# Routing one tile behind its product, and one weight piece of the second layer split on GpSimd, in a fused two-layer kernel on Trainium2

## What is computed

```
x = x + ffn0(cond0(x, c))        # layer 0
x = x + ffn1(cond1(x, c, side))  # layer 1
cond0: per batch a 64x64 channel mix, a softmax-weighted sum of 8 matrices, plus a bias
ffn0 : y @ W0.T + LoRA of the top 2 of 8 experts. The gate is
       h = relu(layernorm(y @ gw1.T + gb1)); g = h @ gw2.T + gb2; top 2, softmax of the two.
       An expert that more than 1536 of the 4096 rows choose (first, or second) is switched off.
cond1: grouped convolution over positions (9 taps, 4 groups) plus a context bias
ffn1 : y @ W.T + b + 8 low-rank experts weighted by a softmax of q.k
```

## Time and profile before

| what | value |
|---|---|
| median of three runs | 1320.56 us (1319.37 to 1320.86) |
| the profiled execution | 1316.55 us, span 1314.8 us |
| TensorE busy | 1285.5 us, 98% of the span |
| VectorE, ScalarE, GpSimd busy | 737.5, 279.8, 236.4 us |
| mean granted clock of TensorE | 0.992 of 2.4 GHz |
| DMA queue q1 | 142.25 MB, 40.8% of 16 engines' span |

### The profile page before, as it was taken

How to read it: one execution, slowest core, us unless ns; L and a number is a source line. 1 busy time by engine, 2 the same in 40 slices (tenths; PEclk the granted TensorE clock), 3 DMA queues, 4 the chain that set the end, 5 groups by cost and what they waited for, 6 DMA issues and landing times.

```text
span 1314.8 us, 20627 instructions
## 1 busy us (share of the span) xinstructions
PE 1285.5 (98%) x7223; PEld 1195.6 (91%) x7223; DVE 737.5 (56%) x1727; ACT 279.8 (21%) x515; POOL 236.4 (18%) x173
## 2 busy tenths in 40 slices
PE   9699999999999997999999999999999999999999
PEld 9699999999999996898998998898898898898897
DVE  6878777777777775644444444444444444344332
ACT  6233222223222332311111111111111111111110
POOL 2344232223222311110100100110110110110110
PEclk9899999999999998999999999999999999999999
DMA  8245534343344347453343353353343343353310
GB/s 295 68 148 164 125 125 125 120 123 105 111 130 114 101 152 215 137 113 74 86 112 73 86 109 77 86 106 79 86 104 81 86 105 81 86 102 84 87 49 32
DMA packets 109879, 142.75 MB, mean 109 GB/s; under 512 B 6160, under 2 KB 86416, under 8 KB 109840
## 3 DMA queue, kind: packets, MB, share of 16 engines
q1 hardware_dynamic: 109840, 142.25, 40.8%
HBM read 88.72 MB, written 53.50 MB: 108 GB/s over the span
## 4 chain that ended last, share of the span: by engine, by line
PE 92%; DVE 4%; DMA 2%; issue 1%; POOL 1%; ACT 0%; SPq 0%; DVEq 0%; POOLq 0%; ACTq 0%
PE ps L1170 28%; PE ps L1172 27%; PE ps L1171 27%; PE ps L1311 6%; PE ps L1312 2%; DMA staging<-in_w 1%; DMA x_round<-whole 1%; DVE oh_all L927 0%; DMA z<-in_cpack 0%; DMA row<-in_xr 0%; PE ps L1402 0%; DVE part L896 0%; DVE row L904 0%; POOL xo L596 0%; PE ps L1287 0%
## 5 line engine op out<-in xcount | busy, mean ns | idle before, releaser
L1170 PE MATMUL ps<-weights,lhs_h 128*128 128x512 f32 (+2 forms) x1408 | 498.5, 354 | 0.8 <-issue 0.8
L1172 PE MATMUL ps<-weights,lhs_l 128*128 128x512 f32 (+2 forms) x1408 | 490.2, 348 | 0.0
L1171 PE MATMUL ps<-weights,lhs_h 128*128 128x512 f32 (+2 forms) x1408 | 489.1, 347 | 0.0
L1170 PEld LDWEIGHTS ps<-weights,lhs_h 128*128 128x128 f32 x1408 | 264.7, 188 | 24.0 <-issue 1.1
L1172 PEld LDWEIGHTS ps<-weights,lhs_l 128*128 128x128 f32 x1408 | 264.4, 188 | 20.8
L1171 PEld LDWEIGHTS ps<-weights,lhs_h 128*128 128x128 f32 x1408 | 264.8, 188 | 20.0
L643 POOL TENSOR_TENSOR xo<-row,wsum 128x512 f32<-128x512 f32 x60 | 76.9, 1308 | 663.5 <-DMA out_x<-xo 663.5
L1170 PE MATMUL ps<-weights 128*128 128x396 f32 x384 | 133.4, 347 | 0.1
L1171 PE MATMUL ps<-weights 128*128 128x396 f32 x384 | 132.6, 345 | 0.0
L1172 PE MATMUL ps<-weights 128*128 128x396 f32 x384 | 132.5, 345 | 0.0
L1142 DVE TENSOR_TENSOR xo<-ps,xo 128x512 f32<-128x512 f32 x64 | 43.1, 691 | 148.3 <-PE ps L1172 148.3
(11 more groups left out here) (151 smaller groups left out, 1466.8 us busy)
## 6 DMA issues: line engine op xcount, KB each, us to landing
row<-spill SPq DMA_DIRECT2D x30, 576.0 KB, 5.7
z<-x_round SPq DMA_DIRECT2D x32, 516.0 KB, 3.8
xo<-in_xt SPq DMA_DIRECT2D x32, 512.0 KB, 4.0
out_x<-xo SPq DMA_DIRECT2D x31, 512.0 KB, 2.7
x_round<-row SPq DMA_DIRECT2D x60, 256.0 KB, 5.5
row<-in_xr SPq DMA_DIRECT2D x31, 394.0 KB, 3.5
spill<-row SPq DMA_DIRECT2D x31, 394.0 KB, 4.4
staging<-in_w SPq DMA_DIRECT2D x8, 832.0 KB, 6.3
```

What stands on the lines that cost most here:

```text
L1170: pe.matmul(out_ap, lhs[0], rhs[0], start=first, stop=False, skip_group_check=True)
L1171: pe.matmul(out_ap, lhs[0], rhs[1], start=False, stop=False, skip_group_check=True)
L1172: return pe.matmul(out_ap, lhs[1], rhs[0], start=False, stop=last, skip_group_check=True)
```

## The change

1. In the first phase VectorE and ScalarE route tile t+1 in period t instead of tile t+2. Ahead of the first period only tile 0 is routed. Periods 0 and 1 have an order of their own. In period 24 two tiles, 25 and 26, are routed, and from then on again tile t+2 in period t.
2. SP loads the first part of row t+3 in period t (before: of row t+4), once tile t+1 is routed.
3. In the turn piece N1+4 is split low by GpSimd, behind its first additions of the second phase, and no longer by VectorE. ScalarE makes its high part behind `z_high(0)` instead of before `y_high(30,2)`. SP issues x1_store(0) before `y01[1]` and piece N1+4 before x1_store(1).

```diff
+        CATCH_UP = 24
+        def routed_in(t):
+            if isinstance(t, int) and t >= CATCH_UP:
+                return [t + 1, t + 2] if t == CATCH_UP else [t + 2]
+            return [t + 1]
-        by_pool = (N_LB0, N_CONV, N_LB1, N1)
+        by_pool = (N_LB0, N_CONV, N_LB1, N1, N1 + 4)
 # SP, ahead of the first period
             for u in range(2):
                 sp.wait_ge(mix_read[0], u + 1)
                 spill0(u, u)
-                sp.wait_ge(spilled0[u], 16)
-                sp.wait_ge(counted, u + 1)
-                load_xr0(u + 2, u)
+            sp.wait_ge(spilled0[0], 16)
+            sp.wait_ge(counted, 1)
+            load_xr0(2, 0)
 # SP, phase_a
                 spill0(t + 2, u)
-                if before_end(t, 4):
-                    left, = counts((it + 2) * 16)
-                    sp.wait_ge(spilled0[u], left)
-                    sp.wait_ge(counted, ahead)            # ahead = t + 3
-                    load_xr0(t + 4, u)
+                left, = counts((it + u + 1) * 16)
+                sp.wait_ge(spilled0[1 - u], left)
+                sp.wait_ge(counted, routed)               # routed = t + 2
+                load_xr0(t + AHEAD, 1 - u)
 # SP, the turn
             chunk(N1 + 3)
+            x1_store(0, 0)
             sp.wait_ge(row_ready12, TILES)
             sp.dma_start(y01[1], spill[P:2 * P, ER:ROW]).then_inc(row_in[1], 16)
-            x1_store(0, 0)
             z_load(0, 0, 0)
+            chunk(N1 + 4)
             x1_store(1, 1)
-            chunk(N1 + 4)
 # GpSimd, phase_b, behind its two additions
+                if at(t, 0):
+                    split_lo(N1 + 4)
 # ScalarE: root(1) ahead of the first period goes; phase_a
-                if later(t, 1):
+                if later(t, 2):
                     y_high(t + 2, 0)
                 bias12_of(t + 1)
                 if later(t, 1):
                     y_high(t, 1)
-                root(t + 2)
+                    for r in routed_in(t):
+                        root(r)
                 y_high(t, 2)
                 if before_end(t, XB):
                     x_high(t + XB, b, it + 2)
+                if at(t, 0):
+                    y_high(3, 0)
+                    root(1)
 # ScalarE, the turn
             y_high(TILES - 3, 2)
-            split_hi(N1 + 4)
             y_high(TILES - 2, 2)
             z_high(0)
+            split_hi(N1 + 4)
 # VectorE: route(1, 1) ahead of the first period goes; phase_a
+                if at(t, 0):
+                    mix_matrix(3, 3); y_low(0, 2); evict(0, 0, 1); evict(2, 0, 0); x_low(4, 0)
+                    y_low(3, 0); evict(0, 0, 2); route(1, 1)
+                elif at(t, 1):
+                    y_low(1, 1); mix_matrix(4, 0); route(2, 0); y_low(1, 2); evict(1, 1, 1)
+                    evict(3, 1, 0); x_low(5, 1)
+                else:
                     mix_matrix(t + AHEAD, (b + AHEAD) % XB)
                     y_low(t, 1)
                     evict(t + 2, u, 0)
-                    route(t + 2, u)
+                    for r in routed_in(t): route(r, r % 2)    # in the loop: route(t + 1, 1 - u)
                     y_low(t, 2)
                     evict(t, u, 1)
                     if before_end(t, XB): x_low(t + XB, b)
 # VectorE, the turn
             z_low(0)
             evict(T2, 0, 2)
-            split_lo(N1 + 4)
             conv_read_low(0, 0, 0)
```

More of the change, by code:

```diff
@@ L451, in phase_a @@
                 u = b % 2
-                now, ahead, more = counts(t, t + AHEAD, t + 5)
+                now, routed, ahead, more = counts(t, t + 2, t + AHEAD, t + 5)
                 if later(t, 1):
@@ L463, in phase_a @@
                 spill0(t + 2, u)
-                if before_end(t, 4):
-                    left, = counts((it + 2) * 16)
-                    sp.wait_ge(spilled0[u], left)
-                    sp.sem_inc(passed_sp, 1)
-                    sp.wait_ge(counted, ahead)
-                    sp.sem_inc(passed_sp, 1)
-                    load_xr0(t + 4, u)
+                left, = counts((it + u + 1) * 16)
+                sp.wait_ge(spilled0[1 - u], left)
+                sp.sem_inc(passed_sp, 1)
+                sp.wait_ge(counted, routed)
+                sp.sem_inc(passed_sp, 1)
+                load_xr0(t + AHEAD, 1 - u)
                 if before_end(t, 6):
@@ L747, in _ @@
             bias12_of(0)
-            root(1)
             def phase_a(t, b, it):
-                if later(t, 1):
+                if later(t, 2):
                     y_high(t + 2, 0)
@@ L977, in _, with links_before @@
             route(0, 0)
-            route(1, 1)
-            A_BASE = 2 + AHEAD * MIX_LINKS + (AHEAD - 1) * ROUTE_LINKS
+            A_BASE = 2 + AHEAD * MIX_LINKS + ROUTE_LINKS
             assert links["n"] == A_BASE - 2, links["n"]
+            def links_before(t):
+                caught_up = isinstance(t, int) and t > CATCH_UP
+                return A_BASE + t * A_LINKS + (ROUTE_LINKS if caught_up else 0)
             def phase_a(t, b, it):
                 u = b % 2
-                restart(t * A_LINKS + A_BASE)
-                if later(t, 1):
+                restart(links_before(t))
+                if later(t, 2):
@@ L986, in phase_a @@
                     evict(t - 1, 1 - u, 2)
                     y_low(t + 2, 0)
-                mix_matrix(t + AHEAD, (b + AHEAD) % XB)
-                if later(t, 1):
-                    y_low(t, 1)
-                evict(t + 2, u, 0)
-                route(t + 2, u)
[L993 to L997, removed]
+                if at(t, 0):
+                    mix_matrix(3, 3)
+                    y_low(0, 2)
+                    evict(0, 0, 1)
+                    evict(2, 0, 0)
+                    x_low(4, 0)
+                    y_low(3, 0)
+                    evict(0, 0, 2)
+                    route(1, 1)
+                elif at(t, 1):
+                    y_low(1, 1)
+                    mix_matrix(4, 0)
+                    route(2, 0)
+                    y_low(1, 2)
+                    evict(1, 1, 1)
+                    evict(3, 1, 0)
+                    x_low(5, 1)
+                else:
+                    mix_matrix(t + AHEAD, (b + AHEAD) % XB)
+                    y_low(t, 1)
+                    evict(t + 2, u, 0)
+                    if isinstance(t, int):
+                        for r in routed_in(t):
+                            route(r, r % 2)
+                    else:
+                        route(t + 1, 1 - u)
+                    y_low(t, 2)
+                    evict(t, u, 1)
+                    if before_end(t, XB):
+                        x_low(t + XB, b)
@@ L999, in _ @@
+                assert at(t, CATCH_UP) or links["n"] == A_LINKS, links["n"]
             periods(dve, phase_a)
             T1, T2, T3 = TILES - 3, TILES - 2, TILES - 1
-            restart((TILES - AHEAD) * A_LINKS + A_BASE)
+            restart(links_before(TILES - AHEAD))
             def x1_add(t, u):
@@ L1079, in _ @@
             link(dve.tensor_tensor(oh_all[:, :, 0:E], oh_all[:, :, 0:E], oh_all[:, :, E:2 * E], ALU.add))
-            B_BASE = A_BASE + (TILES - AHEAD) * A_LINKS + links["n"]
+            B_BASE = links_before(TILES - AHEAD) + links["n"]
             gates(0, 0, 0)
```

## The result

| | median us | lowest to highest | runs |
|---|---|---|---|
| before | 1320.71 | 1319.37 to 1324.73 | 4 |
| after | 1305.78 | 1304.31 to 1306.54 | 4 |

The ratio is 0.9881, 95% interval 0.9857 to 0.9904: faster by 14.9 us. Before has here the three runs of above and a fourth. The forecast was 1306.0. But the two profiled executions are only 10.0 us apart (1316.55 and 1306.54, spans 1314.8 and 1304.8). So the point forecast was hit, and what it was built of has to be looked at term by term.

What follows compares the result with a forecast made beforehand. TensorE was taken as bound by two long waits released by VectorE's y_low, small waits and clock falls. Terms 11.0 + 2.5 - 6.9 + 8.0 = 14.6 us off gave 1306.0 us on the median's scale; range 1299 to 1313.

Steps and rivals of the forecast that it cites:

- Start: First tiles: y_low(0,2) ahead of routing 1 removes the 11.9 us wait, less a new 3.4 us wait; 11.0 us gained.
- Tiles 2 to 23: Steady periods: small TensorE waits go as GpSimd's sum runs after the routing; 2.5 us gained, bounds 0 and 3.0.
- R5: Every period: the late row load becomes the gate, 1323 us or more; chance 0.05.
- Catch-up: Tile 24: two routings in one period make TensorE wait 5.5 us, plus 1.4 slow restart; 6.9 us lost.
- Turn: Between phases: two transfers change places and one split changes engine; 8.0 us gained, bounds 4 and 11.
- (b): Turn: y_high(30,2) no longer stands behind the weight piece; mix(30,2) 7.3 us earlier, another 1.3 from the clock.
- Step 4 of the signs: Turn: gap of 2 to 3 us before mix(29,2), none before mix(30,2), second layer 14.6 us earlier, L1061 usual length.
- (c): Turn: piece N1+4 lands about 511, GpSimd's low split ends 516.7, covered; piece N1+6 later, 0.6 us charged.
- (a): Turn: x1_store(0) ahead of y01[1] delays that row and mix(29,2); cost 2.3 us, bounds 0 and 3.
- R1: Turn: y01[1] lands as now and the split stays clear of VectorE; 2.3 us more gain, 1303.7; chance 0.17.
- R2: Turn: GpSimd's long split meets lhs_l, second layer waits up to 3.8 us longer, 1309.8; chance 0.15.
- R3: Start gives less, or catch-up is at its upper bound: 4 to 7 us less, about 1311.5; chance 0.13.

Runs made afterwards that it cites:

- e11: e5 with y_low(t,2) also ahead of the routing in periods 1 and 2, and the eviction and low split behind it reordered; 1296.75 us, 0.9818.
- e5: The changed kernel with period 24 routing tile 25 alone, and period 25 routing tiles 26 and 27; 1297.73 us, 0.9829 of before.
- e3: The changed kernel with y01[1] loaded before x1_store(0), as in the kernel before; 1305.49 us, 0.9879 of before.
- e8: e3 with pieces N1+5 to N1+7 split before the work on tile 2's row, which TensorE takes last; 1307.43 us, 0.9901 of before.
- e10: e3 with only the first half of the columns of pieces N1+5, N1+6 and N1+7 loaded; 1302.28 us, 0.9858 of before.
- before again: The kernel before, unchanged, run and profiled once more; 1320.95 us, 0.9993, profiled span 1319.1 us.
- e1: The kernel before with only the routing part of the change, the turn left as before; 1308.26 us, 0.9903 of before.
- e2: The kernel before with only the turn's part of the change, the routing left as before; 1316.12 us, 0.9958 of before.
- e4: The changed kernel run once more without edits, as reference; 1305.36 us, 0.9875 of before.
- e7: The changed kernel with useless TensorE matmuls added, 28 before mix(1,1,2) and 60 before mix(24,2); 1305.44 us, 0.9886 of before.
- e6: The changed kernel with the low split of piece N1+4 back on VectorE; 1305.56 us, 0.9893 of before.

## Why the prediction was right, and where it was not

**Start, -11.0 forecast, -11.55 seen.** Step by step as foreseen: no gap at 49.07, routing 2 crossed by GpSimd (58.92 to 65.47, 6.5 us where 7.1 was said), a wait of 2.27 where 3.4 was said. What was not foreseen is that the clock falls behind so short a wait. The windows of after that answer to the earlier trace rows, behind the waits at 66, 407 and 498 us (columns as there):

```profile
67.00:70.00 3.00, 3.00 (x11) 3.00 (x10) 2.96 (x6) 0.00 (x0) 1.87 (x1) 0.50 0.61 189
408.00:411.00 3.00, 3.00 (x10) 3.00 (x11) 3.00 (x5) 0.00 (x0) 0.00 (x0) 0.55 0.20 29
500.00:503.00 3.00, 3.00 (x11) 3.00 (x10) 0.60 (x2) 0.00 (x0) 0.00 (x0) 0.50 1.17 236
```

The third number from the right is the clock: 0.50 to 0.55 of 2.4 GHz, and 10 or 11 matmuls in 3 us. The forecast had seen the clock fall only after 4.4 us of idling, in the first stall of before, and charged a slow restart for longer waits alone. The two errors, 1.1 us less wait and 1.6 of slow clock, nearly cancel.

**Tiles 2 to 23, -2.5 forecast, -3.03 seen.** The periods became 14.61 us, and nine of the ten traces with this routing show 316.62 to 316.74 us for the stretch; the small waits are gone. e11 gives a little of it back. The other side (R5) did not come about; the routing's late load cost nothing.

**Catch-up, +6.9 forecast, +5.6 seen.** The two routings took 5.8 and 5.7 us (395.83 to 401.59, 401.63 to 407.31), each with one GpSimd sum inside, as forecast; the wait was 3.94 instead of 5.5, and the slow clock came, 1.6. VectorE in after: begin of the first routing, end of the second, and the `y_low` for which TensorE waited.

```profile
395.83 0.18 DVE L924 BATCH_NORM_STATS2 stats<-row 128x6 f32<-128x32 f32 x1
...
407.13 0.18 DVE L941 TENSOR_TENSOR count<-count,oh_all 128x16 f32<-128x16 f32 x1
407.35 0.57 DVE L908 TENSOR_TENSOR part<-ps,part 128x396 fp32r<-128x396 f32 x1
```

Most of the 1.6 us by which the wait is shorter lies in the first routing: it grew by 1.0 us beside a GpSimd sum of 1.90, and not by the whole of it as forecast. e5 shows that this loss was not bound to the routing's new place, only to doing two in one period.

**Turn, -8.0 forecast, -1.0 seen: the step that failed.** The mechanism of (b) was right: `mix(30,·,2)` no longer waits. Three terms were mis-sized or missing. (Step 4 of the signs has a slip: the 0.6 us of (c) fall behind the second layer's start, so by the terms this start should have come 15.2 us earlier and not 14.6. It came 13.9 earlier, at 513.21.)

(a) `y01[1]` behind x1_store(0): forecast 2.3 us. The row took 9.1 us to land instead of 5.7. VectorE:

```profile
496.56 1.29 DVE L1046 TENSOR_TENSOR biased<-ps,biased 128x512 f32<-128x512 f32 x2 [4.80 <-DMA biased<-spill]
```

The wait before `mix(29,·,2)` rose by 3.4 us to 3.91, and this time the clock fell behind it (0.50, line above): another 2.6 us, since `mix(30,·,2)` came 7.47 us behind it instead of 4.87. Missing in the sum: 1.1 + 2.6.

(c) The pieces and rows behind it, charged with 0.6 us. The queue, in after:

```profile
495.85 0.58 SPq L367 DMA_DIRECT2D staging<-in_w  x1
497.28 0.96 SPq L445 DMA_DIRECT2D x_round<-biased  x2
...
501.02 0.43 SPq L367 DMA_DIRECT2D staging<-in_w  x1
507.18 0.34 SPq L385 DMA_DIRECT2D spill<-row  x1
507.70 0.37 SPq L456 DMA_DIRECT2D z<-x_round  x1
510.66 0.33 SPq L367 DMA_DIRECT2D staging<-in_w  x1
511.69 0.33 SPq L490 DMA_DIRECT2D row<-spill  x1
...
520.16 0.33 SPq L367 DMA_DIRECT2D staging<-in_w  x1
```

And VectorE, which takes what lands in order:

```profile
518.04 0.29 DVE L1059 TENSOR_TENSOR tmpw<-row,oh_all 128x128 f32<-128x128 f32 x1 [2.57 <-DMA row<-spill]
518.25 1.89 DVE L883 TENSOR_TENSOR weights<-staging,weights 128x1664 fp32r<-128x1664 f32 x1
...
526.14 1.89 DVE L883 TENSOR_TENSOR weights<-staging,weights 128x1664 fp32r<-128x1664 f32 x1 [0.78 <-ACT weights L673]
```

How full the queue was over this stretch, in after (columns as in the earlier trace rows; the last three numbers are clock, DMA share and GB/s):

```profile
485.00:519.00 34.00, 29.25 (x160) 27.81 (x159) 17.97 (x26) 12.89 (x16) 8.78 (x4) 0.90 0.90 247
```

Before, the same stretch has a share of 0.61 and 165 GB/s. The row of tile 2, issued at 511.69, landed 6.3 us later; behind it VectorE freed piece N1+5's buffer at 520.1, only then could N1+7 be issued (520.16), and its low part was ready at 528.03. TensorE waited 2.26 us, with a slow clock behind it: 3.9 us in all (791.59 against 787.66), 3.3 more than charged. Together 1.1 + 2.6 + 3.3 = 7.0, which is what is missing between 8.0 and 1.0.

The last of these is put down to the queue as a whole by three runs: another order of the loads moves the wait from one place to another (e3), another order of the work behind them moves it again (e8), and fewer bytes shorten it (e10). An estimate agrees in size: 1.2 MB at the 247 GB/s of the row above are 4.9 us, and e10 gained 3.5 in its trace. But 2.36 us of wait stay there, and one trace pair with overlapping intervals is thin ground: that the bytes in the queue set the length of the turn is likely, and not shown in full. The forecast had priced the transfers one by one and not as a sum. One profiled pair understates the turn, though: with the old turn three traces (before, before again, e1) took 837.7, 839.1 and 839.3 us, with the new one six (after, e2, e4, e5, e7, e11) 835.0 to 836.7, so some 3 us; the medians of e2 say 5.2.

**The scale, and luck.** The forecast took the difference between the median of before and its profiled execution for a constant. It was chance: the second one of before lies 4.3 higher. Against that one after is 14.3 us shorter, nearly what the medians say, and the stretches give -13.3 at the start (forecast -11.0), -4.2 in tiles 2 to 24 (-2.5), +5.7 in the catch-up (+6.9) and -2.5 in the turn (-8.0). The medians of the halves say the same: the routing brought 13.0 us by itself, twice the 6.6 of the sum, and the turn 5.2 instead of 8.0. So the mechanisms of the routing were right and their worth was put too low, the turn's was put too high, and that the total came out within 0.3 us is luck.

**The rivals.** R1 fell: `y01[1]` did not land as before. R2 did not come about in after, by a margin of 0.9 us: GpSimd's split ran 506.85 to 510.64, `lhs_l` (L1097) began at 511.53 and took 1.48. In e3 the split came 2.8 us earlier and `lhs_l` 4.7, and they met; the cost was 0.7 us, not up to 3.8, since only the last microsecond of the split overlapped. GpSimd and VectorE of e3:

```profile
504.07 3.79 POOL L608 TENSOR_TENSOR weights<-staging,weights 128x1664 fp32r<-128x1664 f32 x1 [13.85 <-ACT weights L673]
```

```profile
505.51 0.69 DVE L1090 TENSOR_TENSOR whole<-ps,bias_in 128x512 f32<-128x512 f32 x1 [0.25 <-PE ps L1347]
506.24 0.69 DVE L1093 TENSOR_TENSOR whole<-ps,whole 128x512 f32<-128x512 f32 x1
506.85 2.17 DVE L1097 TENSOR_TENSOR lhs_l<-whole,lhs_h 128x512 fp32r<-128x512 f32 x2
```

The two reads with an input in PSUM kept their 0.69 us beside the split, and the instruction that reads SBUF alone waited it out. The Trainium skill, page "SBUF — State Buffer", section "SBUF: two separate sides", has the lock between the engines for such SBUF inputs; the trace agrees. R3 and R4 (a poorer start, a cheap catch-up) did not come about.

## What to carry to other kernels

Where a wait goes in a stretch whose DMA queue is nearly full, add up the transfers up to the next thing that the critical engine needs: in the two other orders tried here the wait came back at another transfer of the same queue, and only fewer bytes shortened it. Catch up on postponed work over several periods, into the idle time of each, and not in one; here that was worth 6 to 8 us, about half of what the whole change brought. Price a step by more than one profiled execution when the terms are 1 to 4 us, and never carry the offset between one execution and the median over to another kernel.

## What the runs showed of the hardware

The granted clock fell to 0.50 behind waits far shorter than the first stall suggested. Behind gaps (from the start of one matmul to the start of the next) at 66 us of 2.18, 2.25, 2.31, 2.33 and 2.61 us it fell (e4, e5, e10, e8, after), behind gaps of 2.05, 2.14 and 2.28 us it did not (e3, e1, e6). Before `mix(29,·,2)` it fell with a wait of 2.84 us (e7) and stayed at 1.00 with one of 3.09 (e5), where `mix(30,·,2)` followed 4.97 us behind. So the length of the wait alone does not decide it. In this kernel a wait of about 2.2 us puts 1.6 us at stake, and that is part of the spread between executions.

The stores x1_store(0) into HBM (512 KB) hold back what is in the queue with them: y01[1] (512 KB) landed after 9.1 us behind x1_store(0) and after 5.8 us ahead of it, and an 832 KB piece issued ahead of both after 7.7 and 4.4 us. Whether their bytes or their small rows do it, no run here separates.
